# Two layers of a graph network on one core: three tables of partial neighbour sums in place of four, and a neighbour loop of six groups

## The reference

```python
def _L0_gnn_ref(embeddings, edge_row, edge_col, edge_val, W1, W2):
    gathered = embeddings[edge_col] * edge_val[:, None]
    relevant = jax.ops.segment_sum(gathered, edge_row, num_segments=N_NODES)
    non_interactive = relevant @ W1
    interactive = relevant * embeddings @ W2
    return non_interactive + interactive
...
x = _layernorm(x + _L0_gnn_ref(x, src, dst, edge_weight, W1, W2))
x = _layernorm(x + _L1_gnn_ref(x, edge_attr_64, ..., edge_index))
```

## Time and profile before

| | us |
|---|---|
| time before, median of 3 runs | 13406.58 |
| the 3 runs | 13405.91 to 13411.36 |
| span of the profiled execution, first to last instruction | 13260.2 |
| median less span (launch and end, outside the trace) | 146.4 |
| busy in the span: PE, DVE, ACT, POOL | 7727.7, 5558.1, 3368.4, 8204.5 |

### The profile page before, as it was taken

The page is one execution under the profiler, slowest core; times in us unless marked ns, Lnnn a source line. Parts: engine busy times, 40 slices in busy tenths (PEclk is TensorE's granted clock), DMA queues, the critical chain, the costliest instruction groups (busy, mean ns, idle before and its releaser), DMA issues. The chain is left out here.

```text
span 13260.2 us, 210680 instructions
## 1 busy us (share of the span) xinstructions
PE 7727.7 (58%) x48566; PEld 6102.5 (46%) x48566; DVE 5558.1 (42%) x20556; ACT 3368.4 (25%) x7806; POOL 8204.5 (62%) x6569
## 2 busy tenths in 40 slices
PE   2444444444444444444577777777777777777777
PEld 1344333334344334333355555555555555555555
DVE  2333333333333333334544444444444454444455
ACT  1111111111111111111233333333333333333333
POOL 3888888888888888886344444444444444444441
PEclk7666666666666666666777777777777777777776
DMA  8666666666666666666555555555555555555552
GB/s 197 106 106 106 106 105 106 106 105 106 106 106 106 106 106 106 106 106 130 182 137 138 139 137 138 136 140 140 138 137 138 138 139 139 140 137 138 137 138 76
DMA packets 2236565, 1660.60 MB, mean 125 GB/s; under 512 B 734074, under 2 KB 1994684, under 8 KB 2236252
## 3 DMA queue, kind: packets, MB, share of 16 engines
q0 software_dynamic: 628992, 668.10, 30.1%
q1 hardware_dynamic: 1538069, 907.12, 24.7%
q10 hardware_dynamic: 69448, 84.72, 1.9%
HBM read 1374.49 MB, written 284.45 MB: 125 GB/s over the span
## 5 line engine op out<-in xcount | busy, mean ns | idle before, releaser
L467 POOL DMA_INDIRECT rel_sum<-sums,row x3224 | 5004.5, 1552 | 1193.1 <-issue 631.8
L1058 POOL DMA_INDIRECT kv<-kv_rows,src_idx x3232 | 3121.7, 966 | 3420.8 <-DVE msg L1280 2494.2
L423 PE MATMUL coef_ps<-same,spread 128*128 128x128 f32 x6448 | 1640.6, 437 | 3528.6 <-DVE spread L396 2914.6
L423 PEld LDWEIGHTS coef_ps<-same,spread 128*128 128x128 f32 x6448 | 1424.2, 325 | 3711.0 <-DVE spread L396 3078.8
L1298 DVE TENSOR_TENSOR acc<-acc,out_ps 128x256 f32 x3232 | 1364.4, 422 | 1946.9 <-remote 911.2
L410 DVE TENSOR_TENSOR row<-moved,src_col 128x8 int32<-128x8 f32 x403 | 69.5, 173 | 3760.8 <-DMA rel_sum<-sums,row 3760.7
L1091 PE MATMUL ring_ps<-pick,q_win 128*128 128x128 f32 x6464 | 1265.6, 351 | 141.6 <-issue 134.3
L1091 PEld LDWEIGHTS ring_ps<-pick,q_win 128*128 128x128 f32 x6464 | 1075.8, 249 | 583.2 <-issue 574.4
L1149 PE MATMUL out_ps<-put,msg 128*128 128x128 f32 x6464 | 1236.2, 350 | 3.8 <-issue 3.8
L396 DVE TENSOR_SCALAR spread<-iota_n,rel_col,w_col 128x128 f32<-128x128 f32 x3224 | 1214.5, 382 | 0.0
L392 DVE SCALAR_TENSOR_TENSOR same<-src_bc,src_col,later 128x128 f32<-128x128 f32 x3224 | 1118.2, 347 | 202.0 <-issue 136.5
(11 more groups left out here) (164 smaller groups left out, 7310.4 us busy)
## 6 DMA issues: line engine op xcount, KB each, us to landing
q_win<-q_rows SPq DMA_DIRECT2D x3232, 64.0 KB
src_bc<-src_flat SPq DMA_DIRECT2D x403, 512.0 KB
x_win<-in_x SPq DMA_DIRECT2D x3224, 64.0 KB
rel<-rel_flat SPq DMA_DIRECT2D x404, 256.0 KB
attr<-in_edge_attr SPq DMA_DIRECT2D x804, 128.0 KB
mark<-marks ACTq DMA_DIRECT2D x202, 256.0 KB
kv<-kv_rows,src_idx POOLq DMA_INDIRECT x3232
rel_sum<-sums,row POOLq DMA_INDIRECT x3224
```

The costliest lines, as they stand in the source:

```text
L423: last = nc.tensor.matmul(coef_ps[k][:, i, :], spread[:, b, j, :], same[:, b, j, :], start=True, stop=True)
L467: pool.indirect_dma_start(out=rel_sum[r], out_offset=bass.IndirectOffsetOnAxis(ap=row[:, b, j:j + 1], axis=0), in_=sums[:, b, j, :], in_of ...
L1058: pool.indirect_dma_start(out=kv[:, 2 * i + u, k * S + s, :], out_offset=None, in_=kv_rows, in_offset=bass.IndirectOffsetOnAxis(ap=src_idx ...
```

## The change

`REPLICAS` goes from 4 to 3, and `UNROLL`, 2 before, is 6, the smallest number of whole groups above two whose tiles are a multiple of three. Three edits follow. The table of a tile is now counted over the loop's body and not in the group (`adds` works out how many tiles before it went to its table, and `rows_landed` waits for the same groups as before). `prepare` zeroes three tables, with 21 DMAs in place of 28. `nodes_one` loads three parts of `rep` a block and adds them with two DVE instructions in place of three; SP's wait before it loads into `rep` again is on the product (`summed`) and not on the half sums (`halved`). The head of the neighbour loop is six groups, its tail one, and the loop turns 66 times.

```diff
-REPLICAS = 4
+REPLICAS = 3
...
-        PER = G // REPLICAS
+        UNROLL = 6
+        assert UNROLL * G % REPLICAS == 0
+
+        def adds(s, j, r):
+
+            return s.u * (UNROLL * G // REPLICAS) + (s.k * G + j - r + REPLICAS - 1) // REPLICAS
+
+        def rows_landed(eng, s):
+
+            if isinstance(s.u, int) and s.k < 2:
+                return
+            for r in range(REPLICAS):
+                wait(eng, added[r], 16 * adds(s.plus(-1), 0, r))
...
-                steps(sp, NG, 2, 2, 1, body)
+                steps(sp, NG, UNROLL, UNROLL, (NG - UNROLL) % UNROLL, body)
...
-                    for r in range(REPLICAS):
-                        wait(dve, added[r], 16 * PER * (s.g - 1))
+                    rows_landed(dve, s)
...
-                        r, before = j % REPLICAS, j // REPLICAS
+                        r = (s.k * G + j) % REPLICAS
                         if j % 4 == 0:
                             pool.wait_ge(sum_out, s.g * 2 + j // 4 + 1)
 
-                        wait_alone(pool, added[r], (s.g * PER + before) * 16, passed)
+                        wait_alone(pool, added[r], 16 * adds(s, j, r), passed)
...
-        half_sum = sb("half_sum", [P, 2, 4 * D])
+        half_sum = sb("half_sum", [P, 1, 4 * D])
...
-                    wait_alone(sp, halved, 2 * (s.g - 1), passed)
+                    wait_alone(sp, summed, 2 * (s.g - 1), passed)
...
-                    nc.vector.tensor_tensor(half_sum[:, 1, :], rep[:, b, 2, :], rep[:, b, 3, :], ALU.add
-                                            ).then_inc(halved, 1)
-                    dve.wait_ge(halved, 2 * (s.g + 1))
+                    dve.wait_ge(halved, s.g + 1)
                     wait(dve, pair_turned, 2 * (s.g - 1))
                     nc.vector.tensor_tensor(pair[:, b, 0].rearrange("p j d -> p (j d)"), half_sum[:, 0, :],
-                                            half_sum[:, 1, :], ALU.add).then_inc(summed, 1)
+                                            rep[:, b, 2, :], ALU.add).then_inc(summed, 1)
```

More of the change, by code:

```diff
@@ L407, in body @@
                     dve.wait_ge(rows_b, s.g + 1)
-                    for r in range(REPLICAS):
-                        wait(dve, added[r], 16 * PER * (s.g - 1))
+                    rows_landed(dve, s)
                     nc.vector.tensor_tensor(row[:, b, :], moved[:, b, :], src8, ALU.add).then_inc(rows, 1)
-                steps(dve, NG, 2, 2, 1, body)
+                steps(dve, NG, UNROLL, UNROLL, (NG - UNROLL) % UNROLL, body)
             @block.tensor
@@ L434, in body @@
                         last.then_inc(sum_done, 1)
-                steps(pe, NG, 2, 2, 1, body)
+                steps(pe, NG, UNROLL, UNROLL, (NG - UNROLL) % UNROLL, body)
             @block.scalar
@@ L446, in body @@
                                              ).then_inc(coef_out, 1)
-                    for r in range(REPLICAS):
-                        wait(act, added[r], 16 * PER * (s.g - 1))
+                    rows_landed(act, s)
                     for k in range(2):
@@ L452, in body @@
                                              ).then_inc(sum_out, 1)
-                steps(act, NG, 2, 2, 1, body)
+                steps(act, NG, UNROLL, UNROLL, (NG - UNROLL) % UNROLL, body)
             @block.gpsimd
@@ L470, in body @@
                             bounds_check=N + P - 1).then_inc(added[r], 16)
-                steps(pool, NG, 2, 2, 1, body)
+                steps(pool, NG, UNROLL, UNROLL, (NG - UNROLL) % UNROLL, body)
                 for r in range(REPLICAS):
-                    pool.wait_ge(added[r], 16 * PER * NG)
+                    pool.wait_ge(added[r], 16 * adds(Step(0, NG, UNROLL), 0, r))
 class Chain:
```

## The result

The changed kernel took 13530.92 us, median of 4 runs (13520.59 to 13540.60); beside it on the same chip the kernel before took 13406.24, median of 4 (13402.13 to 13411.36). The ratio is 1.0096, with a 95% interval from 1.0084 to 1.0107: slower by 125 us.

A forecast was written before the change was run, and what follows sets the result against it. POOL's issue of accumulating DMAs was taken to bound the neighbours stage. Span 13260.2 + 242 (stall) - 14 (zeros) - 15 (sums) = 13473; on the median, 13406.6 + 213 = 13620 us, range 13430 to 13720.

The forecast's parts named there:

- half the stall: Rival in the neighbours stage: group patterns go on taking turns, or needed lead is about 0.5 us; 13539 us, chance 0.17.
- POOL's issue rate as the bound: In the neighbours stage POOL issues a tile's add each 1.857 us with no slack; any delay there delays the end.
- The lead and the fourth tile back: POOL's sequencer waits for tile i-4; with three tables its lead over the engine shrinks 1.85 us, where 0.9 is wanted.
- Which groups pay: In the neighbours loop 335 of 403 groups meet the broadcast at tile 3, paying 0.7 us; the other 67 pay 0.1.
- Term 1: In the neighbours stage POOL stalls at tile 6, waiting for tile 3's late landing: +242 us.
- Term 2: In prepare, a quarter of the zeros is not written, so SP's chain goes on earlier: 14 us saved.
- Term 3: In nodes_one, one table sum fewer saves 0.60 us a block in 24 of 25 blocks: 15 us saved in all.
- Hidden or nothing: Unrolled head, wait values and 134 fewer loop turns in neighbours cost nothing; bounds 160 us lost, 15 gained.
- The rule that spoke against term 1: A POOL DMA of 64 KB takes 2.15 us, so no lead in neighbours is ever short and term 1 is 0.

The follow-up runs named there:

- e3: Loop of six groups with four tables as before, against the kernel before: 10861.90 us, ratio 0.9986; again on another chip 13291.15 us, ratio 1.0007.
- e2: The changed kernel run again without an edit, against the kernel before on the same chip: 11013.59 us, ratio 1.0129.
- e1: The kernel before run again without an edit, for a second trace: 10873.78 us, ratio 0.9999 against itself.

## Why the prediction was right, and where it was not

The direction, the mechanism and the place held; the forecast of 13620 was 89 us too high. The time lies inside the range of 13430 to 13720, but 29 us below the 13560 to 13690 of the forecast itself, in the range of the rival called half the stall (13430 to 13560). The range held because it was drawn over the rivals too.

**POOL's issue rate as the bound.** Held. The whole growth of the stage is idle time of POOL: 1328.3 - 191.8 = 1136.5 us behind the first tile against 1193.1 - 209.9 = 983.2 before (191.8 and 209.9 are the wait ahead of the first tile), 153 us more; busy time is 4.8 less (4999.7 for 5004.5), and the two together are the 148 us from first to last add.

**The lead and the fourth tile back.** Held. With three tables the lead at the stage's end is 2.1 us for 4.1, and a tile that waits for one that landed in 5.5 us stalls. The e3 run shows such late landings without the stall when the wait is one tile further back.

**Which groups pay.** Held. Late groups are those without a turn of the loop ahead: in the middle one of them the broadcast comes 1.3 us behind tile 3, and 1.7 in the middle one of the 67 behind a turn. The rival "half the stall" had two conditions. The first, that the patterns go on taking turns, is refuted: what came out at its size is the full number of groups at a lower price. The second, a needed lead of about 0.5 us, was nearer the truth: the lead is 0.75, between that and the forecast's 0.9.

**Term 1 was mis-sized:** 242 predicted, 148 measured (165 in e2). With 7 us given to the groups behind a turn, (148 - 7) / 335 = 0.42 us a group, (165 - 7) / 335 = 0.47 in e2, in place of 0.7. Added up from POOL's timeline it is 0.43 and 0.47 in the 335 groups, and the 7 us for the groups behind a turn held (6.8 and 6.2 before tile 7). Two things make up the difference, and both can be read over all groups, with the landing of tile 3 taken from the MOVE of the tile that waits for it, as the prediction did at four.

- The lead needed is 0.75 us, the least that any add behind the first group has in either trace of the changed kernel, and not the 0.9 that I read on the idle engine at the first tile. In the trace of before the odd groups' landings cost 0.71 us a group at a lead of 0.9 and 0.57 at 0.75. So the 0.7 taken from four landings, three of them alike, was right for the kernel before, by luck more than by the size of the sample; the lead is worth 0.14.
- The landings did not stay as they were. In the odd groups of before 11% of tile 3's DMAs land within 4.8 us, early enough for no stall; with six groups and four tables (e3) it is 18%, and in the changed kernel it is 28% (29% in e2). That takes the price from 0.57 to 0.43 (0.47 in e2). The prediction had said that the phase stays and the stall repeats in each group; it repeats in about seven of ten. Why tile 3 lands early more often isn't shown.

So the price of a group is no constant. At six late-type groups of the changed kernel tile 6 stood idle for 0.54 us more than the usual 0.30 (at 972.40), for nothing (987.21), 0.79 (1714.69), 0.74 (3253.17), 0.63 (4699.46) and 0.14 (5503.52). A wait with a threshold turns every spread in the landing into such a mixture.

**Term 2, the zeros:** 14 predicted; `prev_t` was read 14.8 us earlier in the first measurement and the stage began 17.7 earlier, in e2 13.8. Held.

**Term 3, the sums:** 15 predicted; from the last add to the first gather e2 is 16.8 shorter. Held, with PE's slack where it was said to be: in the block without a sum ahead DVE waits 1.61 us for `y_ps`, 1.60 before.

```profile
6537.62 0.69 DVE L592 TENSOR_TENSOR y<-xb,y_ps 128x512 f32<-128x512 f32 x1 [1.61 <-PE y_ps L657]
```

**Hidden or nothing.** Held. The e3 run has the longer loop with 134 turns less, and a stage of 5982.0 for 5985.1. The wait values worked out at every third tile are not in it, but in the changed kernel the idle time above the usual 0.30 adds up to no more than 3 us over the stage before any of the tiles 0 to 5.

**A step that was wrong,** without changing the forecast: that the 146.4 us between the trace's span and the median of the runs are launch and end, "which nothing here changes". After, the profiled run's time is 1.7 us above its span, and the kernel before has 1.6 in e1. What the two traces of the first measurement show in place of launch and end is a shorter attention stage in the profiled execution of before: its gathers take 6525.5 us there, 6671.8 after (6586.2 to 13258.0), 146.3 more, while on one chip both kernels take 4151.1 and 4152.2. So the difference goes with the execution and not with the change, as far as one trace of each can tell; read against the trace of before alone, the span of after (+258.7) would have been put down to the change at twice its cost.

**The rule that spoke against term 1.** The two-table run decides it by the time. If an add landed 2.15 us after its start, then with a lead of 0.75 a tile could start 2.9 us after the one it waits for, well under two tiles of 1.85, and two tables would have cost nothing; they cost 1337 us in this stage (7321.8 for 5985.1). The 2.15 us are an estimate for 64 KB from the figure in the Trainium skill, page "DMA: Bandwidth & Descriptors", section "Anatomy of one DMA — SWDGE (gpsimd) path", and no trace here agrees with it. The same section of the Trainium skill says that the issuing sequencer waits before dispatch, which agrees with all the MOVE rows here.

## What to carry to other kernels

A DMA-issuing engine that shows only its usual gap may stand one buffer away from a stall: read the lead of its sequencer over the engine, compare it with the lead needed by an engine in work (not by an idle one), and subtract one tile's time before taking a buffer away. Look for the large transfer that some groups meet and others don't, and for the loop turn that decides it; that phase is part of the price. Price a wait at a threshold with the mean over many landings, and don't count on the landings to stay as they were under the change. Compare stages on one chip before blaming a change for the rest of the span.

## What the runs showed of the hardware

- An add whose sequencer has just been released starts 0.75 us after its MOVE when the engine was at work just before (3252.4 to 3253.17, 3835.1 to 3835.88); the first of the stage takes 0.9 (193.8 to 194.7). No add behind the first group of either trace of the changed kernel has less than 0.75.
- An accumulating DMA of 64 KB lands 3.3 us after its start in the middle case (e1). A broadcast of 512 KB delays it by when it is issued: over seven traces, with the landing read from the MOVE of the waiting tile, nine in ten of tile 3's DMAs land at 4.4 to 5.8 us when the broadcast comes 1.2 to 1.5 us behind their start, and at 3.3 to 4.1 us when it comes 1.5 us or more behind; then the next tile is delayed, by less. Halving the broadcast's bytes at the same number of packets gave no shorter stage (6175.0, 6150.5). What sets the delay wasn't found.
- The attention stage took 4.15 ms on some chips and 6.5 to 6.7 on others, at a granted clock of 1.00 and 0.78 in the same stretch, and on the latter 146 us apart between two executions of the same gathers. The stage bound by POOL's issue took 5982 to 5987 us with four tables in the four traces, on chips of either kind.
